# One transfer, two issuers: the row of the maxima leaves from ScalarE instead of SyncE in an attention and feed-forward kernel

## The chip, the cores and the metric

The kernel runs on one core of a Trainium2 chip. The metric is the device time of one execution in microseconds. A program is timed over whole executions; the profile shows one of them, with the span from its first to its last instruction. Five engines work side by side, each with its own order of instructions: TensorE (PE), VectorE (DVE), ScalarE (ACT), GpSimd (POOL) and SyncE (SP), which here only issues transfers. They wait for each other through semaphores.

## The reference, cut to what matters

```python
def layernorm(x): return (x - mean(x)) / sqrt(var(x) + 1e-5)

def attention(x, W_qkv, b_qkv, W_out, b_out):      # x: 32 x 256 x 128 (batch, position, feature)
    q, k, v = split(x @ W_qkv + b_qkv)             # 16 query heads and 4 key/value heads of 8
    scores = einsum('bkgsd,bktd->bkgst', q, k) / sqrt(8)   # 4 query heads share one key head
    scores = where(causal, scores, -inf)
    return (softmax(scores) @ v) @ W_out + b_out

def ffn(x, weight, alpha, bias):                   # weight made ternary: -1, 0, 1
    return x @ (ternary(weight) * alpha).T + bias

x = x + layernorm(attention(layernorm(x)))
x = x + layernorm(ffn(layernorm(x)))
```

## The kernel before

The 32 batch elements ("batches") are taken one after the other, each with 256 positions of 128 features in two halves of 128 rows. The stages of a batch are spread over many steps: each engine has a function `step(t)` that lists, in a fixed order written by hand, the pieces of work that it does in step t, for batches of different age (`exp(t - 3, 0)`, `norm(t - 8, ...)`). Each piece starts with the semaphores that it waits for. Nothing else sets the order: an engine, and the queue of the transfers that it issues, goes through its list from top to bottom.

What a batch b goes through, as far as it matters here:

1. ACT copies the turned input from PSUM (`xn1T`, L488). PE makes queries and keys of it (L916), ACT takes them with their bias (`QK`, L495 and L496).
2. Queries and keys are cut into three bfloat16 parts (`part1` on ACT, L456; `rest` on GpSimd, L400; `part2` on ACT, L463; `part3` on GpSimd, L378), and SP sends these parts into the stacks `QS` and `KS` (L260 and L270), six transfers for QS and three for KS a batch. Four batches have stacks of their own (`RING = 4`).
3. PE multiplies the stacks once for the maxima (`mx`, L846); DVE reduces them (`maxima`, L627) to the largest score of each query within a head. DVE and GpSimd make a high and a low bfloat16 part of it (`Mp`, L690 and L392), PE turns them (`turn`, L886), and ACT copies the result to `MpT` (`take_turned`, L470). MpT is a single buffer of 16 x 512.
4. A transfer, `send_max` (L278), puts MpT, 16 KB, into the last two rows of the stack QS. With those rows the scores product gives scores with the maxima already subtracted.
5. PE makes the scores (`st`, L795); its first piece for a batch waits for `s_mrow`, the semaphore of that transfer. ACT takes the exponentials (`exp`, PT, L427), PE multiplies them by the values (`pv`, L819), ACT copies the sums (`Y`, L449).
6. The divisors: SP sends them out of Y to `den` (L286), DVE inverts them (`rec`, L699), SP stores them to DRAM (`rec_dram`, L294) and loads them back, spread over the rows (`rden`, L301, 256 KB). GpSimd multiplies (`yn`, L386), PE makes the output product (L875), DVE adds the bias and takes the moments.
7. The attention's layer norm is applied by ACT in place of DVE (`norm(b, 1, ...)`, A, L440, two instructions of 128 x 128), with a shift and a scale that GpSimd computes (`shift`, L362). The feed-forward part follows later (x3, ff, `norm(b, 3, ...)`, F, the same line).

SP's order around the maxima is `load_x`, `spread_rec`, `send_max`, then the remaining parts of Q and K. So `send_max` stands behind the load of rden, which waits until rec_dram has landed. ACT's order at the end of a step is the exponentials 3 and 4, `take_turned(t - 2)`, the norm of A, and then, at the head of the next step, `take_xn1`.

`take_turned` waits for `s_mrow` before it overwrites MpT, and signals `s_mt`, for which the transfer waits. A helper `free` (L208) makes the waits that keep a buffer from being overwritten; each is an instruction of its own on the engine's sequencer.

Of the kernel before, what the change touches and what calls it, by code (L numbers as in the profile page):

```python
# [23 lines left out]
MAXROW = BL + PARTS  # L24
# [4 lines left out]
RING = 4  # L29
# [7 lines left out]
def on(b):  # L37

    return 0 <= b < B
# [23 lines left out]
def build(nc, x, wq, wk, wv, wo, bq, bk, bo, wf, alpha, bf, ident, qfix, kfix, vmask, bvw, out):  # L63
    with ExitStack() as ctx:
        def sb(name, shape, dt):
            return ctx.enter_context(nc.sbuf_tensor(name, shape, dt))
# [4 lines left out]
        def sem(name):  # L71
            return ctx.enter_context(nc.semaphore(name))
# [37 lines left out]
        QS = [sb(f"QS{i}", [128, NH, S], BF16) for i in range(RING)]  # L110
# [4 lines left out]
        MpT = sb("MpT", [4 * NKV, 2 * S], BF16)  # L115
# [62 lines left out]
        s_mt = sem("s_mt")  # L178
        s_mrow = sem("s_mrow")
# [43 lines left out]
        def _(sp):  # L223
# [17 lines left out]
            def load_x(t):  # L241
                g = t + 1
                if g < B // GRP:

                    sp.wait_ge(s_x, g * 16)
                    load(g)
# [6 lines left out]
            def q_rows(b, part, c):  # L253
                if on(b):
                    i = b % RING
                    src = (part1, part2, part3)[part][i]

                    sp.wait_ge((s_p1, s_p2, s_p3)[part], b + 1)
                    r = BL + HD * c
                    sp.dma_start(QS[i][r:r + HD, :, :], src[:, 0, :]).then_inc(s_stack[i], 16)  # L260
# [10 lines left out]
                                 src[0:32 * n, 1, :].unsqueeze(1).broadcast_to([32 * n, COPIES, S]))\  # L271
                      .then_inc(s_stack[i], 16)

            def send_max(b):
                if on(b):

                    sp.wait_ge(s_mt, b + 1)
                    sp.dma_start(QS[b % RING][MAXROW:MAXROW + 2, :, :], MpT[:]).then_inc(s_mrow, 16)  # L278

            def send_den(b):  # L280
                if on(b):
                    i = b % 2

                    sp.wait_ge(s_y, b + 1)
                    free(sp, b, s_rec, bufs=2)
                    sp.dma_start(den[i][:], Y[i][HD:128:2 * HD].rearrange("r a s -> r (a s)")).then_inc(s_den[i], 16)  # L286
# [9 lines left out]
            def spread_rec(b):  # L296
                if on(b):
                    i = b % 2

                    second(sp, b, s_recd[i])  # L300
                    sp.dma_start(rden[i][:].rearrange("r a s -> r (a s)"),  # L301
                                 rec_dram[i].unsqueeze(1).broadcast_to([8, 16, NLO * S])).then_inc(s_shift[i], 16)
# [12 lines left out]
            def step(t):  # L315
                load_x(t)
                spread_rec(t - 5)
                send_max(t - 3)
                q_rows(t - 1, 1, 1)
                q_rows(t - 1, 1, 5)  # L320
                k_rows(t - 1, 2)
                q_rows(t - 1, 2, 0)
                store_x(t - 21)
                send_den(t - 4)
                rows_free(t)
                q_rows(t, 0, 2)
                q_rows(t, 0, 3)
                q_rows(t, 0, 4)
                store_rec(t - 4)
                k_rows(t, 0)  # L330
                k_rows(t, 1)

            for t in range(B + 21):
                step(t)
# [82 lines left out]
        @block.scalar  # L417
        def _(act):
            def exp(b, n):
                if not on(b):  # L420
                    return
                banks = ST_CHUNKS[n][2]

                act.wait_ge(s_st_ps, CHUNKS * b + n + 1)
                if b * CHUNKS + n >= TILES:
                    act.wait_ge(s_pv, CHUNKS * b + n - TILES + 1)
                nc.scalar.activation(PT[(b * CHUNKS + n) % TILES][:, 0:512 * banks],  # L427
                                     ps_st[n % 2][:, 0:banks, :].rearrange("p a c -> p (a c)"),
                                     ACT.Exp, scale=SCALE).then_inc(s_exp, 1)

            def norm(b, k, src, dst, done, added):

                if not on(b):
                    return

                i = b % 2
                act.wait_ge(s_rstd[k], 3 * b + 3)
                free(act, b, added, bufs=2)
                for j in range(TT):
                    last = nc.scalar.activation(dst[i][:, j, :], src[i][:, j, :], ACT.Identity, bias=shift[k][i][:, j:j + 1],  # L440
                                                scale=rstd[k][i][:, j:j + 1])
                last.then_inc(done, 1)

            def take_y(b):
                if on(b):

                    act.wait_ge(s_pv, CHUNKS * b + CHUNKS)
                    free(act, b, s_yn, bufs=2)
                    nc.scalar.copy(Y[b % 2][:], ps_y[:]).then_inc(s_y, 1)  # L449

            def first_part(b):
                if on(b):

                    act.wait_ge(s_qk, 2 * b + 2)
                    stack_sent(act, b, RING)
                    nc.scalar.copy(part1[b % RING][:], QK[:]).then_inc(s_p1, 1)  # L456

            def second_part(b):
                if on(b):

                    act.wait_ge(s_r1, b + 1)
                    stack_sent(act, b, RING)
                    nc.scalar.copy(part2[b % RING][:], rest[:]).then_inc(s_p2, 1)  # L463

            def take_turned(b):
                if on(b):

                    act.wait_ge(s_mt_ps, b + 1)
                    free(act, b, s_mrow, 16)
                    nc.scalar.copy(MpT[:].rearrange("r (h i s) -> r i h s", h=2, i=NB),  # L470
                                   ps_w[0:16, :].rearrange("r (i h s) -> r i h s", i=NB, h=2)).then_inc(s_mt, 1)


            def take_v(b):
                if on(b):

                    act.wait_ge(s_v_ps, b + 1)
                    free(act, b, s_pv, CHUNKS, RING)
                    nc.scalar.copy(VB[b % RING][:, :, 0:HD],
                                   ps_w[:, 0:128].rearrange("p (n c) -> p n c", c=HD)).then_inc(s_vb, 1)  # L480

            def take_xn1(b):
                if on(b):

                    act.wait_ge(s_xt_ps, b + 1)
                    free(act, b, s_v_ps)
                    free(act, b, s_qk_ps)
                    nc.scalar.copy(xn1T[:], ps_w[:, 0:S]).then_inc(s_xt, 1)  # L488

            def take_qk(b):  # L490
                if on(b):

                    act.wait_ge(s_qk_ps, b + 1)
                    free(act, b, s_r1)
                    nc.scalar.activation(QK[:, 0, :], ps_w[:, 0:S], ACT.Identity, bias=bq_sb[:, 0:1]).then_inc(s_qk, 1)  # L495
                    nc.scalar.activation(QK[:, 1, :], ps_w[:, S:2 * S], ACT.Identity,  # L496
                                         bias=bk_sb[:, 0:1]).then_inc(s_qk, 1)

            def take_xn3(b):
                if on(b):  # L500

                    act.wait_ge(s_x3_ps, b + 1)
                    free(act, b, s_ff_ps)
                    nc.scalar.copy(xn3T[:], ps_w[:, 0:S]).then_inc(s_x3, 1)

            for dst, src in ((id_sb, ident), (wk_sb, wk), (bq_sb, bq), (bk_sb, bk)):
                act.dma_start(dst[:], src).then_inc(s_early, 16)
            for dst, src in ((wv_sb, wv), (vm_sb, vmask)):
                act.dma_start(dst[:], src).then_inc(s_vconst, 16)
            for dst, src in ((wo_sb, wo), (bv_sb, bvw), (bo_sb, bo)):  # L510
                act.dma_start(dst[:], src).then_inc(s_late, 16)
            act.wait_ge(s_setg, 1)
            for i in range(RING):
                act.dma_start(KS[i][MAXROW:ROWS], neg[:].unsqueeze(1).broadcast_to([2, NKV, KLEN])).then_inc(s_neg, 16)

            act.wait_ge(s_early, EARLY)
            def step(t):
                take_xn1(t)
                exp(t - 4, 5)
                take_qk(t)  # L520
                take_y(t - 4)
                take_xn3(t - 7)
                first_part(t)
                exp(t - 3, 0)
                take_v(t)
                exp(t - 3, 1)
                exp(t - 3, 2)
                norm(t - 8, 3, F1, F2, s_f2, s_fin)
                second_part(t)
                exp(t - 3, 3)  # L530
                exp(t - 3, 4)
                take_turned(t - 2)
                norm(t - 5, 1, A1, A2, s_a2, s_x1)

            for t in range(B + 8):
                step(t)
# [488 lines left out]
```

## Time and profile before

| | us |
|---|---|
| median of 3 runs | 444.55 (444.14 to 447.34) |
| the profiled execution's own time | 445.07 |
| its span | 442.9 |
| PE busy | 374.9 (85%) |
| DVE busy | 359.0 (81%) |
| ACT busy | 329.3 (74%) |
| POOL busy | 300.2 (68%) |

The profiled execution is 0.52 us above the median. Between its span and its own time lie 2.2 us. A batch takes some 11 to 12 us in the middle of the kernel; the first batches and the last ones, where the stages fill and drain, have other limits.

In what follows PEq, ACTq and SPq are the sequencers of the engines: they issue transfers and carry out waits, and their time isn't counted as busy. PEld is the weight load of TensorE, which runs beside its products.

### The profile page before, as it was taken

The page shows a single profiled execution, that of the slowest core. Times are in us where ns is not written, and L with a number is a line of the kernel's source. Part 1 is how long each engine was busy: PE and PEld are TensorE (multiplying, and loading weights), DVE is VectorE, ACT ScalarE, POOL GpSimd, SP SyncE. Part 2 cuts the span into 40 slices and gives each one's busy share as a digit, 9 for nine tenths or more (in the row PEclk, how much of TensorE's full clock was granted, in tenths as well). Part 3 has the DMA queues.
Part 4 walks back from the last instruction along what each step waited for, and adds up shares of the span by engine and source line. Part 5 has one row for each costly group of instructions (what it writes and reads, how often), then busy time and mean ns, then how long its engine had stood idle before and what let it go on. Part 6 is the DMA issues. An engine that isn't in the chain of part 4 may idle for free.

```text
span 442.9 us, 19241 instructions
## 1 busy us (share of the span) xinstructions
PE 374.9 (85%) x7430; PEld 279.5 (63%) x7430; DVE 359.0 (81%) x1148; ACT 329.3 (74%) x609; POOL 300.2 (68%) x584
## 2 busy tenths in 40 slices
PE   0617897999999889999999999999999998798631
PEld 0414676777667667777777767777677776575320
DVE  5378784989989898998999989898899987785542
ACT  0412784888888888898988989898888998668521
POOL 2423332667877777787887878887787777556765
PEclk9967996999999999999999999999999999999865
DMA  5275542454544444433334334443444343311151
GB/s 148 39 89 73 95 88 64 108 107 108 109 106 98 96 104 107 87 80 85 74 83 90 72 88 96 85 105 82 95 87 107 84 108 83 90 30 57 48 170 47
DMA packets 72530, 39.58 MB, mean 89 GB/s; under 512 B 13272, under 2 KB 68280, under 8 KB 72440
## 3 DMA queue, kind: packets, MB, share of 16 engines
q1 hardware_dynamic: 71104, 37.70, 39.9%
q8 instruction: 59, 0.97, 1.0%
q10 hardware_dynamic: 1336, 0.66, 0.6%
q14 instruction: 31, 0.25, 0.2%
HBM read 13.67 MB, written 4.72 MB: 42 GB/s over the span
## 4 chain that ended last, share of the span: by engine, by line
PE 34%; DMA 30%; SPq 11%; DVE 8%; issue 7%; ACT 6%; POOL 3%; POOLq 0%; ACTq 0%; DVEq 0%
DMA QS<-MpT 15%; PE ps_st L795 8%; PE ps_mx L846 7%; DMA den<-Y 7%; PE ps_y L819 7%; DMA rec_dram<-rec 5%; SPq L270 4%; PE ps_w L875 3%; PE ps_w L916 3%; SPq L260 3%; DVE M L627 3%; ACT PT L427 2%; PE ps_w L905 2%; SPq L301 2%; DMA QS<-part 1%
## 5 line engine op out<-in xcount | busy, mean ns | idle before, releaser
L627 DVE TENSOR_REDUCE M<-ps_mx 128x2 f32<-128x512 f32 (+3 forms) x352 | 212.0, 633 | 26.0 <-PE ps_mx L846 25.5
L427 ACT ACTIVATE PT<-ps_st 128x1024 f32<-128x1024 f32 (+1 forms) x192 | 162.6, 884 | 27.3 <-PE ps_st L795 21.6
L846 PE MATMUL ps_mx<-KS,QS 112*64 112x128 bf16 (+2 forms) x2560 | 137.0, 225 | 12.8 <-DMA QS<-part 6.7
L846 PEld LDWEIGHTS ps_mx<-KS,QS 112*64 112x64 bf16 x2560 | 94.0, 112 | 46.7 <-DVE M L627 16.8
L795 PE MATMUL ps_st<-QS,KS 114*64 114x256 bf16 (+1 forms) x1024 | 103.6, 304 | 17.4 <-DMA QS<-MpT 16.8
L358 POOL TENSOR_TENSOR rstd<-vareps,mhalf 128x2 f32<-128x2 f32 x128 | 91.8, 717 | 10.0
L819 PE MATMUL ps_y<-PT,VB 128*32 128x256 f32 (+3 forms) x2048 | 90.5, 303 | 0.4 <-ACT PT L427 0.3
L795 PEld LDWEIGHTS ps_st<-QS,KS 114*64 114x64 bf16 x1024 | 48.5, 111 | 24.5 <-DMA QS<-MpT 22.0
L819 PEld LDWEIGHTS ps_y<-PT,VB 128*32 128x32 f32 x2048 | 49.7, 109 | 12.8 <-issue 6.1
L386 POOL TENSOR_TENSOR yn<-Y,rden 128x512 f32<-128x512 f32 x32 | 40.7, 1270 | 15.8 <-DMA rden<-rec_dram 15.6
L592 DVE BATCH_NORM_STATS2 stats<-X 128x6 f32<-128x128 f32 x128 | 30.7, 281 | 23.8 <-POOL X L370 12.0
L400 POOL TENSOR_TENSOR rest<-QK,part 128x512 f32<-128x512 f32 x32 | 37.1, 1159 | 13.8 <-ACT part L456 13.7
L610 DVE TENSOR_SCALAR xn<-X,mv,rstd 128x128 f32<-128x128 f32 x128 | 40.8, 359 | 3.1 <-PE ps_w L896 2.8
L356 POOL TENSOR_TENSOR vareps<-mv,eps 128x2 f32<-128x2 f32 x128 | 25.4, 198 | 24.2 <-DVE mv L602 23.9
L875 PE MATMUL ps_w<-wo_sb,yn 128*64 128x128 f32 x512 | 36.1, 287 | 4.3 <-POOL yn L386 4.1
L392 POOL TENSOR_TENSOR Mp<-M,Mp 128x32 bf16<-128x32 f32 x32 | 7.8, 245 | 45.1 <-DVE Mp L690 45.0
L378 POOL TENSOR_TENSOR part<-rest,part 128x512 bf16<-128x512 f32 x32 | 37.1, 1159 | 1.5 <-ACT part L463 1.5
L440 ACT ACTIVATE A<-A,shift,rstd 128x128 f32<-128x128 f32 x64 | 28.1, 485 | 11.6 <-POOL shift L362 10.8
L495 ACT ACTIVATE QK<-ps_w,bq_sb 128x256 f32<-128x256 f32 x32 | 15.2, 475 | 26.8 <-PE ps_w L916 26.8
L875 PEld LDWEIGHTS ps_w<-wo_sb,yn 128*64 128x64 f32 x512 | 29.6, 145 | 5.2 <-POOL yn L386 5.1
L602 DVE BATCH_NORM_AGGREGATE mv<-stats 128x2 f32<-128x6 f32 x256 | 30.8, 162 | 0.7
L440 ACT ACTIVATE F<-F,shift,rstd 128x128 f32<-128x128 f32 x64 | 28.0, 491 | 3.5 <-POOL shift L362 3.5
(63 smaller groups left out, 489.7 us busy)
## 6 DMA issues: line engine op xcount, KB each, us to landing
QS<-part SPq DMA_DIRECT2D x192, 64.0 KB
rden<-rec_dram SPq DMA_DIRECT2D x32, 256.0 KB
X<-in_x SPq DMA_DIRECT2D x15, 256.0 KB, 4.4
out<-X SPq DMA_DIRECT2D x15, 256.0 KB, 3.8
KS<-part SPq DMA_DIRECT2D x32, 96.0 KB
KS<-part SPq DMA_DIRECT2D x32, 64.0 KB
KS<-part SPq DMA_DIRECT2D x32, 32.0 KB
QS<-MpT SPq DMA_DIRECT2D x32, 16.0 KB
```

Of the source, the lines that this page charges most:

```text
L358: gp.tensor_tensor(rstd[k][i][:], vareps[k][i][:], mhalf[:], ALU.pow).then_inc(s_rstd[k], 1)
L378: gp.tensor_tensor(part3[i][:], rest[:], part2[i][:], ALU.subtract).then_inc(s_p3, 1)
L386: gp.tensor_tensor(yn[i][:], Y[i][:], rden[i][:], ALU.mult).then_inc(s_yn, 1)
L400: gp.tensor_tensor(rest[:], QK[:], part1[b % RING][:], ALU.subtract).then_inc(s_r1, 1)
L427: nc.scalar.activation(PT[(b * CHUNKS + n) % TILES][:, 0:512 * banks], ps_st[n % 2][:, 0:banks, :].rearrange("p a c -> p (a c)"), ACT.Exp, ...
L440: last = nc.scalar.activation(dst[i][:, j, :], src[i][:, j, :], ACT.Identity, bias=shift[k][i][:, j:j + 1], scale=rstd[k][i][:, j:j + 1])
L610: last = nc.vector.tensor_scalar(dst[i][:, j, :], src(j), mv[k][i][:, j, 0:1], rstd[k][i][:, j:j + 1], ALU.subtract, ALU.mult)
L627: nc.vector.tensor_reduce(M[b % 2][:].rearrange("p k g i -> p (k g) i")[:, 2 * kv:2 * kv + pairs, i], ps_mx[(b * BANKS + n) % 2][:, 0:pair ...
L795: last = pe.matmul(dst[64 * hi:64 * hi + 64, SLOT * slot:SLOT * (slot + nj)], k[:, 2 * hi + lo, key_block(i, diag), :], q[:, j:j + nj, h:h ...
L819: last = pe.matmul(ps_y[32 * g:32 * g + 32, lo, BL * i:S], v[:, at:at + 2, :].rearrange("p a c -> p (a c)"), p[:, g, slot:slot + NB - i, : ...
L846: last = pe.matmul(ps_mx[(b * BANKS + n) % 2][64 * one:64 * one + 64, at:at + w], q[:, h, BL * i:BL * i + BL], k[:, kv, blocks, :], start= ...
L875: last = pe.matmul(ps_w[h:h + 64, D * j:D * j + D], y[:, lo, 128 * j + h:128 * j + h + 64], wo_sb[:, lo, :], start=(lo == 0), stop=(lo == ...
```

## The change

`send_max` goes from SP's program to ACT's. In SP's step it is taken out between `spread_rec(t - 5)` and `q_rows(t - 1, 1, 1)`. In ACT's step it is added as the last piece, behind the norm of A: in the same step in which ACT copies MpT, with the two instructions of the norm between the copy and the transfer. Its wait (`s_mt`), its bytes, its destination and its semaphore stay as they are. No other piece moves.

```diff
@@ SP
-            def send_max(b):
-                if on(b):
-
-                    sp.wait_ge(s_mt, b + 1)
-                    sp.dma_start(QS[b % RING][MAXROW:MAXROW + 2, :, :], MpT[:]).then_inc(s_mrow, 16)
-
@@ SP, step
                 load_x(t)
                 spread_rec(t - 5)
-                send_max(t - 3)
                 q_rows(t - 1, 1, 1)
                 q_rows(t - 1, 1, 5)
                 k_rows(t - 1, 2)
@@ ACT
+            def send_max(b):
+                if on(b):
+
+                    act.wait_ge(s_mt, b + 1)
+                    act.dma_start(QS[b % RING][MAXROW:MAXROW + 2, :, :], MpT[:]).then_inc(s_mrow, 16)
@@ ACT, step
                 take_turned(t - 2)
                 norm(t - 5, 1, A1, A2, s_a2, s_x1)
+                send_max(t - 2)
```

ACT's order after the change, from the copy of one batch's MpT to the copy of the next Y (names as above, the engine's waits in brackets, the numbers at the end are shapes):

```order
L463 CAST MpT<-ps_w 16x4x2x64 [waits s_mrow,s_mt_ps]
L433 ACTIVATE A_0<-A_0,shift_0,rstd_0 128x128 [waits s_x1,s_rstd1]
L433 ACTIVATE A_0<-A_0,shift_0,rstd_0 128x128
L471 DMA QS<-MpT 2x8x512 [waits s_mt]
L487 COPY xn1T<-ps_w 128x256 [waits s_qk_ps,s_v_ps,s_xt_ps]
L420 ACTIVATE PT<-ps_st 128x512 [waits s_pv,s_st_ps]
L494 ACTIVATE QK<-ps_w,bq_sb 128x256 [waits s_r1,s_qk_ps]
L495 ACTIVATE QK<-ps_w,bk_sb 128x256
L442 COPY Y<-ps_y 128x512 [waits s_yn,s_pv]
```

The same piece before the change:

```order
L470 CAST MpT<-ps_w 16x4x2x64 [waits s_mrow,s_mt_ps]
L440 ACTIVATE A_0<-A_0,shift_0,rstd_0 128x128 [waits s_x1,s_rstd1]
L440 ACTIVATE A_0<-A_0,shift_0,rstd_0 128x128
L488 COPY xn1T<-ps_w 128x256 [waits s_qk_ps,s_v_ps,s_xt_ps]
L427 ACTIVATE PT<-ps_st 128x512 [waits s_pv,s_st_ps]
```

Only the row of the transfer is new; the line numbers differ for the same work because a function moved in the file.

SP's order before the change, from the store of one batch's inverted divisors to the sending of the next den:

```order
L294 DMA rec_dram<-rec 128x32 [waits s_yn,s_rec]
L270 DMA KS<-part_3 24x8x256 [waits s_p1]
L270 DMA KS<-part_3 16x8x256 [waits s_p2]
L231 DMA X<-in_x 128x4x128 [waits s_x]
L301 DMA rden<-rec_dram 128x1x512 [waits s_recd1]
L278 DMA QS<-MpT 2x8x512 [waits s_mt]
L260 DMA QS<-part_3 8x16x256 [waits s_p2] x2
L270 DMA KS<-part_3 8x8x256 [waits s_p3]
L260 DMA QS<-part_3 8x16x256 [waits s_p3]
L286 DMA den<-Y 128x1x32 [waits s_rec,s_y]
```

After it:

```order
L288 DMA rec_dram<-rec 128x32 [waits s_yn,s_rec]
L270 DMA KS<-part_3 24x8x256 [waits s_p1]
L270 DMA KS<-part_3 16x8x256 [waits s_p2]
L231 DMA X<-in_x 128x4x128 [waits s_x]
L295 DMA rden<-rec_dram 128x1x512 [waits s_recd1]
L260 DMA QS<-part_3 8x16x256 [waits s_p2] x2
L270 DMA KS<-part_3 8x8x256 [waits s_p3]
L260 DMA QS<-part_3 8x16x256 [waits s_p3]
L280 DMA den<-Y 128x1x32 [waits s_rec,s_y]
```

The maxima no longer stand between the load of rden and the second parts of Q; the rest keeps its order.

## Rows read from the trace of the kernel before

**Rows 1.** Waits of the whole span: engine, line, releaser, us in total, times, longest
```profile
PE ps_st L795 <- DMA QS<-MpT: 16.8, 19, 2.7
```

**Rows 2.** The page, part 4: the chain that ended last, by line, share of the span
```profile
DMA QS<-MpT 15%; PE ps_st L795 8%; PE ps_mx L846 7%; DMA den<-Y 7%; PE ps_y L819 7%; DMA rec_dram<-rec 5%; SPq L270 4%; PE ps_w L875 3%; PE ps_w L916 3%; SPq L260 3%; DVE M L627 3%; ACT PT L427 2%; PE ps_w L905 2%; SPq L301 2%; DMA QS<-part 1%
```

**Rows 3.** Waits of the stretch 89.91 to 367.20 us, columns as in the first group
```profile
ACT QK L495 <- PE ps_w L916: 12.7, 24, 0.7
...
PE ps_st L795 <- DMA QS<-MpT: 8.8, 14, 1.4
...
DVE rec L699 <- DMA den<-Y: 5.9, 10, 1.4
...
ACT A L440 <- POOL shift L362: 0.3, 1, 0.3
```

**Rows 4.** Busy time by stretch (from the end of one copy of MpT to another)
```profile
core 0: us, PE busy (x) PEld busy (x) DVE busy (x) ACT busy (x) POOL busy (x), PEclk, DMA share, GB/s
241.66:252.53 10.87, 10.86 (x238) 8.52 (x232) 10.57 (x36) 9.99 (x20) 9.25 (x19) 1.00 0.38 84
252.53:264.49 11.96, 11.07 (x236) 8.51 (x232) 10.53 (x36) 10.13 (x21) 9.12 (x19) 1.00 0.32 79
...
89.91:367.20 277.29, 266.91 (x5576) 202.79 (x5568) 252.60 (x826) 243.16 (x455) 218.68 (x424) 1.00 0.43 94
```

**Rows 5.** Timeline of ACT, 241 to 244 us: start, duration, line, output<-input, idle before
```profile
241.10 0.56 ACT L470 CAST MpT<-ps_w 16x512 bf16<-16x512 f32 x1
241.56 0.88 ACT L440 ACTIVATE A<-A,shift,rstd 128x128 f32<-128x128 f32 x2
242.35 0.37 ACT L488 COPY xn1T<-ps_w 128x256 f32<-128x256 f32 x1
...
243.99 0.47 ACT L495 ACTIVATE QK<-ps_w,bq_sb 128x256 f32<-128x256 f32 x1 [0.52 <-PE ps_w L916]
```

**Rows 6.** Timeline of PE in the same batch: its first scores product
```profile
245.56 0.60 PE L795 MATMUL ps_st<-QS,KS 114*64 114x256 bf16 x6
```

**Rows 7.** The chain, 184 to 208 us; the last row is ACT's timeline
```profile
188.94 3.28 DMA den<-Y
...
192.63 2.96 DMA rec_dram<-rec
...
195.60 0.62 SPq L301
...
196.26 4.33 DMA QS<-MpT
...
195.26 0.56 ACT L470 CAST MpT<-ps_w 16x512 bf16<-16x512 f32 x1
```

**Rows 8.** The page, part 6: transfers of 16 KB, median us to landing at the end
```profile
rec_dram<-rec SPq DMA_DIRECT2D x32, 16.0 KB, 2.0
```

**Rows 9.** Timeline of SP in the batch of the fifth group
```profile
241.68 0.67 SPq L278 DMA_DIRECT2D QS<-MpT  x1
```

**Rows 10.** The wait of L208 in 264.30 to 264.38 us; timeline of ACT there
```profile
L208 ACTq EVENT_SEMAPHORE  x1: 38/38/38, 264.3 to 264.3; - x1
...
263.93 0.56 ACT L470 CAST MpT<-ps_w 16x512 bf16<-16x512 f32 x1
264.39 0.87 ACT L440 ACTIVATE A<-A,shift,rstd 128x128 f32<-128x128 f32 x2
265.35 0.37 ACT L488 COPY xn1T<-ps_w 128x256 f32<-128x256 f32 x1
```

**Rows 11.** Timeline of ACT and SP at the kernel's start: issues only
```profile
0.74 0.45 ACTq L507 DMA_DIRECT2D id_sb<-in_ident  x1
...
5.18 3.27 ACTq L514 DMA_DIRECT2D KS<-neg  x4
...
0.74 0.45 SPq L233 DMA_DIRECT2D X<-in_x  x1
```

**Rows 12.** Timeline of POOL and PE, 258 to 261 us
```profile
258.65 1.27 POOL L386 TENSOR_TENSOR yn<-Y,rden 128x512 f32<-128x512 f32 x1 [1.54 <-DMA rden<-rec_dram]
...
259.98 1.09 PE L875 MATMUL ps_w<-wo_sb,yn 128*64 128x128 f32 x16
```

## The prediction

> **What bounds the kernel now.** I read the waits, the chain, the busy times of two neighbouring batches, and then one batch in the timeline. Shares of the span say little where four engines hand the same batch to each other, so the first look is at who ends the idle time. TensorE stood still for 16.8 us in 19 places at L795, the scores product, for one transfer: QS<-MpT, the row of the maxima [rows 1]. That transfer is also 15% of the chain [rows 2]. This is the object of the change, and it is a real wait.
>
> How much of it is steady state? In the stretch 89.91 to 367.20 us there are 24 batches (ACT waits once in each for the query product, 24 times), and 8.8 of the 16.8 us lie there, in 14 waits [rows 3]. The windows give the price of one: a batch without it lasted 10.87 us, the next one, with it, 11.96 us; the mean of the 24 is 277.29 / 24 = 11.55 us [rows 4]. In the short batch PE is busy 10.86, DVE 10.57 and ACT 9.99 us of 10.87 [rows 4], so about 10.9 us is a floor that a cheaper transfer can't break.
>
> The reader should then see a batch at close range. ACT ends the copy of MpT at 241.10 + 0.56 = 241.66 us, the norm of A runs behind it until 242.44, and xn1T begins at 242.35, without a gap [rows 5]. TensorE comes to the first scores product at 245.56, which is 3.90 us after the copy's end [rows 6]. That is the due time of the transfer: whatever lands later than copy + 3.9 stops TensorE, and behind it ACT's first exponential.
>
> The transfer misses it for two reasons, both to be seen in one piece of the chain [rows 7]. First the issue: den<-Y, the reciprocal, rec_dram<-rec and then the SP issue of L301 (rden) run until 196.22, and only then does SP issue the maxima, at 196.26, though their copy ended at 195.82. The maxima stand in SP's order behind a load that waits for another chain. The same difference, taken from the two rows of each of the 32 batches, adds up to about 10 us; in half of them it is under 0.05. Second the landing: 4.33 us for 16 KB, when the same number of bytes of rec_dram<-rec has a median of 2.0 us [rows 8]. Ahead of the maxima on SP's queue lie the 256 KB of rden, issued 0.66 us before.
>
> **The change part by part.**
> Removed from SP: 32 issues of 0.67 us [rows 9], of a batch of 11.5 us. SP isn't waited for in most of that time, so I cost the relief at nothing by itself; what it moves (the parts of Q and K, then den<-Y, all up to 0.7 us earlier) can only help the den chain.
>
> Issue time. ACT's transfer waits for ACT's own copy, and for SP's neighbour no more. It stands behind both instructions of the norm. Does the sequencer reach it only when they have ended, 0.8 us after the copy, or before? The trace shows it for another instruction in the same place: the wait of L208 that stands behind both norm instructions and ahead of xn1T ran at 264.3 us [rows 10], while the copy of that batch ran to 264.49 and the norm began at 264.39. So ACT's sequencer is ahead of its engine by the norm, and I take the issue at copy + 0.05, as early as SP's best (241.66 to 241.68 [rows 5, 9]). If the norm's shift from GpSimd is late, the transfer is late with it; a wait of the norm for the shift was large enough to be listed once in 24 batches, with 0.3 us [rows 3].
>
> Landing time. No trace of this kernel shows this transfer on ACT's queue with rden on the other. The bounds are 2.0 us (rec_dram<-rec, [rows 8]) and 4.33 (the same transfer now, [rows 7]). I take 3.2, in the middle: the 256 KB no longer stand in front, but the same engines move them. Landing is then at copy + 0.05 + 3.2 = copy + 3.25, ahead of the 3.90 of TensorE. At 4.33 it would be copy + 4.4, half a microsecond late in every batch.
> The Trainium skill, DMA: Bandwidth & Descriptors, section Issuing engines are not separate DMA queues, speaks against the gain in landing: transfers of all issuers interleave on the same engines, and another issuer saves only issue time. By that alone the landing stays near 4.3, and the result is the third case below; the lower row of 2.0 us doesn't decide it, since nothing large was ahead of that transfer.
>
> Gain: all 8.8 us of the steady waits, which leaves 11.55 - 8.8 / 24 = 11.2 us a batch, above the floor; and of the 16.8 - 8.8 = 8.0 us in the ramps half, 4.0, since other waits stand beside them there. Together 12.8 us.
>
> Cost on ACT. An issue of this kind takes about 0.65 us of the sequencer: 0.67 on SP [rows 9], and on ACT the four small KS<-neg took 3.27 us, waits included, so at most 0.82 each [rows 11]. It hides under the norm, 0.88 us in the engine [rows 5]: from copy + 0.05 to copy + 0.73, then the waits of xn1T. xn1T now begins 0.69 us after the copy in the short batch (242.35 - 241.66), so it slips by some 0.1 to 0.15 in these, and not at all where it begins at copy + 0.86 (265.35 - 264.49 [rows 10]), as it does in about half of the batches. 30 batches x 0.07 = 2 us, all on the path: qk follows xn1T, and ACT is nearly dense from there on. If the cover were gone the price would be 0.67 + 0.04 = 0.71 us a batch.
> At the kernel's start ACT and SP issue side by side, 0.45 us each from 0.74 on [rows 11], so I add nothing for a collision of the two issuers. The Trainium skill, Perfetto Trace Analysis, section DMA Instruction - HWDGE, says that the block that makes descriptors is locked for one sequencer at a time; if ACT had to wait out an issue of SP, about 0.6 us more would stand on ACT, which is near the price without cover.
>
> What is late next: rden itself. In one slow batch GpSimd waited 1.54 us for it and began yn at 258.65; TensorE's L875 followed at 259.98, straight behind its 1.27 us [rows 12]. With the batch shortened by 0.9 us that chain would stop TensorE instead. Four of the 24 batches look like this, some also wait for den (5.9 us of DVE in all [rows 3]). I give back 2 us.
>
> Sum: - 12.8 + 2.0 + 2.0 = - 8.8 us. The profiled execution took 445.07 us, so 436.3; it lies 0.5 above the median of 444.55, which gives 435.8, say 436.
>
> **The rivals.**
> *The den chain takes over.* SP no longer gates the maxima, but den, rec, rec_dram and rden still run one after the other: 3.28 + 2.96 us in transfers alone [rows 7]. If each shortened batch meets it, only a third of the 12.8 is left: - 4 us, 440.5. For it: DVE waited for den in 10 of the 24 batches [rows 3]. Against: in the short batches this chain was in time, and its transfers now leave earlier.
> *The landing stays.* With 4.33 us the transfer wins only the delay of its issue. Batch by batch that is worth the smaller of the delay and of TensorE's wait; I took both from the timeline for the batches with a wait and got 7.5 us; less 2 on ACT is - 5.5: 439.
> *More than forecast.* The den chain gets faster too and the batches come to 11.0: 24 x 0.55 + 4 + some = - 15: 430. All ramps gone as well gives 424 at the very least; I stop at 429.
> *Slower: ACT stands still for its issue.* If ACT's engine gets nothing while its sequencer issues, or the issue comes only after the norm, 0.71 us lie between norm and xn1T in every batch. ACT has no slack there: it is busy without a gap from the copy to xn1T, and its idle time before QK, 0.52 us [rows 5], waits for a product of xn1T and moves with it. 29 x 0.71 = 20.6 against 12.8 is + 8; by the floor, 11.0 + 0.71 against 11.55, it is + 4 in the steady part. Between them + 6: 450.5. It decides from about 0.36 us a batch on, where 30 of them eat the net 10.8. For it: no ACT row shows an issue between two activations. Against: the wait that ran ahead of the norm [rows 10].
>
> **How the numbers follow.** Forecast as summed 50%, more 8%, landing stays 15%, den chain 12%, slower 15%. The likeliest gives 436. The range 429 to 444 leaves out the slower case and a little beneath. One per cent, about what a measurement of this kernel can tell from no change, is 440.1 and 449.0. Faster by more: 50 + 8 + most of the third case + a third of the den case = 0.71; slower by more: most of the last, 0.12; the rest, 0.17, within.
>
> **What the profile after would show.** Right: QS<-MpT issued by ACTq within 0.1 us of the copy's end, while the norm runs; the wait of L795 for it nearly gone from 16.8 us; xn1T at copy + 0.8 to 0.9 everywhere; steady batches of about 11.2 us; and DVE's wait for den or GpSimd's for rden as the largest of the transfers. Wrong: an issue after the norm's end, or xn1T at copy + 1.4, is the slower case; a wait at L795 that stays at 0.5 us in each batch means the queue was not what delayed the landing; batches of 11.4 with more than 15 us of waits for den and rden mean that the bound only moved.

## The result: slower, and the profile after

The changed kernel takes 461.31 us (459.69 to 465.63, 4 runs) against 445.94 us before (444.14 to 447.48): the ratio is 1.044, with an interval of 1.037 to 1.051. The prediction was 436 us, range 429 to 444. The profiled execution took 465.63 us, with a span of 463.5 us. It is the slowest of the four, 4.3 us above their median, so its span grew by 20.6 us where the medians differ by 15.4.

First the wait that was to vanish. The waits of the changed kernel, whole span (engine, line, releaser, us in total, times, longest):

```profile
DVE M L627 <- PE ps_mx L846: 44.7, 50, 2.2
...
ACT PT L420 <- PE ps_st L795: 37.0, 37, 2.5
PE ps_st L795 <- DMA QS<-MpT: 30.4, 28, 2.1
...
POOL yn L379 <- DMA rden<-rec_dram: 14.2, 8, 4.3
```

TensorE now waits 30.4 us for the maxima, not 16.8 [rows 1]. DVE and ACT wait behind it, and the waits for rden haven't grown. In part 4 of the profile's page, the same transfer is a quarter of the chain, instead of 15% [rows 2]:

```profile
DMA QS<-MpT 25%; PE ps_st L795 8%; ACT PT L420 7%; PE ps_mx L846 6%; PE ps_y L819 4%; PE ps_w L875 3%; ACT F L433 3%; DMA QS<-part 2%; ACT MpT L463 2%; PE ps_w L916 2%; SPq L260 2%; PE ps_w L861 2%; POOL rstd L351 2%; PE ps_w L905 1%; DVE M L627 1%
```

The same 24 batches as in [rows 4], again from copy to copy (stretch, us, busy times):

```profile
core 0: us, PE busy (x) PEld busy (x) DVE busy (x) ACT busy (x) POOL busy (x), PEclk, DMA share, GB/s
241.06:252.87 11.81, 11.13 (x238) 8.51 (x232) 10.67 (x36) 10.19 (x20) 9.33 (x19) 1.00 0.39 79
...
93.40:386.75 293.35, 269.62 (x5576) 205.40 (x5568) 255.14 (x825) 244.29 (x455) 219.71 (x424) 0.99 0.44 88
```

293.35 against 277.29 us is 16.1 of the 20.6 us by which the span grew: 12.22 us a batch instead of 11.55. Of the rest, 2.8 us lie between the first copy of MpT and the fifth, and about 2 us behind the last one.

Then one batch at close range, which answers to [rows 5, 9]. ACT's timeline, with its transfer, and SP's of the same time:

```profile
240.50 0.56 ACT L463 CAST MpT<-ps_w 16x512 bf16<-16x512 f32 x1
240.97 0.49 ACT L433 ACTIVATE A<-A,shift,rstd 128x128 f32<-128x128 f32 x1
241.09 0.62 ACTq L471 DMA_DIRECT2D QS<-MpT  x1
241.36 0.48 ACT L433 ACTIVATE A<-A,shift,rstd 128x128 f32<-128x128 f32 x1
241.83 0.37 ACT L487 COPY xn1T<-ps_w 128x256 f32<-128x256 f32 x1
...
239.52 0.62 SPq L295 DMA_DIRECT2D rden<-rec_dram  x1
240.18 1.27 SPq L260 DMA_DIRECT2D QS<-part  x2
241.85 0.72 SPq L270 DMA_DIRECT2D KS<-part  x1
...
245.12 0.63 SPq L280 DMA_DIRECT2D den<-Y  x1
```

The issue on ACT is all that was hoped for: 0.03 us after the copy's end (241.06), between the two instructions of the norm, with xn1T at copy + 0.77. But SP has sent two copies of Q's second part, 128 KB, at 240.18: 0.9 us *ahead* of the maxima. Before, SP waited for the maxima's copy, because it had to send them, and these parts left only behind that. The chain and TensorE's timeline show the end of that transfer:

```profile
241.09 4.75 DMA QS<-MpT
...
245.88 0.62 PE L795 MATMUL ps_st<-QS,KS 114*64 114x256 bf16 x6 [0.68 <-DMA QS<-MpT]
```

Means over the 24 batches, from the records of the issues, of the packets and of the semaphore in the trace: the first copy of Q's second part left 1.00 us after the maxima's copy before, and in none of the 24 ahead of it; now 0.41 us ahead of the copy's end, and in 19 of 24 ahead of or with the maxima. The last packet of the maxima ran 2.72 us after their issue before, 3.78 now. They landed 3.83 us after the issue before, 4.97 now; from the copy, 4.12 before and 5.01 now. The growth lies in the packets: the first one begins 2.57 us after the issue instead of 2.14, and the 16 of them then take 1.21 us from the first start to the last instead of 0.57, with packets of the parts between them; the tail behind the last start hardly changed (1.11 and 1.19). TensorE comes to its first scores product 4.1 us after the copy in the mean of both kernels (3.90 was the batch of [rows 6]); that product began 4.47 us after the copy before and begins 5.11 after it now. These 0.64 us are nearly all of the 0.67 us by which a batch grew.

### The profile page after: what moved, and what is told of

It reads as the page before. It is cut to its first block, busy times and chain, and to the rows that moved or that the text cites. A ratio compares the mean times of both kernels' runs of the same rounds, so it can differ in the third digit from the quotient of the medians.

```text
span 463.5 us, 19241 instructions
## 1 busy us (share of the span) xinstructions
PE 384.8 (83%) x7430; PEld 286.9 (62%) x7430; DVE 361.8 (78%) x1148; ACT 330.6 (71%) x609; POOL 299.5 (65%) x584
## 3 DMA queue, kind: packets, MB, share of 16 engines
HBM read 13.67 MB, written 4.72 MB: 40 GB/s over the span
## 4 chain that ended last, share of the span: by engine, by line
DMA 30%; PE 29%; ACT 14%; issue 12%; DVE 5%; POOL 5%; SPq 3%; POOLq 0%; ACTq 0%; DVEq 0%
DMA QS<-MpT 25%; PE ps_st L795 8%; ACT PT L420 7%; PE ps_mx L846 6%; PE ps_y L819 4%; PE ps_w L875 3%; ACT F L433 3%; DMA QS<-part 2%; ACT MpT L463 2%; PE ps_w L916 2%; SPq L260 2%; PE ps_w L861 2%; POOL rstd L351 2%; PE ps_w L905 1%; DVE M L627 1%
## 5 line engine op out<-in xcount | busy, mean ns | idle before, releaser
L846 PE MATMUL ps_mx<-KS,QS 112*64 112x128 bf16 (+2 forms) x2560 | 139.6, 229 | 11.6 <-DMA QS<-part 6.0
L795 PE MATMUL ps_st<-QS,KS 114*64 114x256 bf16 (+1 forms) x1024 | 106.0, 309 | 30.7 <-DMA QS<-MpT 30.4
L846 PEld LDWEIGHTS ps_mx<-KS,QS 112*64 112x64 bf16 x2560 | 97.7, 115 | 44.8 <-DVE M L627 11.8
L351 POOL TENSOR_TENSOR rstd<-vareps,mhalf 128x2 f32<-128x2 f32 x128 | 90.2, 705 | 10.0
L795 PEld LDWEIGHTS ps_st<-QS,KS 114*64 114x64 bf16 x1024 | 48.6, 113 | 40.9 <-DMA QS<-MpT 38.6
L875 PE MATMUL ps_w<-wo_sb,yn 128*64 128x128 f32 x512 | 37.2, 293 | 5.0 <-POOL yn L379 5.0
L875 PEld LDWEIGHTS ps_w<-wo_sb,yn 128*64 128x64 f32 x512 | 30.8, 149 | 6.0 <-POOL yn L379 5.9
L348 POOL TENSOR_TENSOR nmean<-mv,minus 128x2 f32<-128x2 f32 x64 | 12.7, 199 | 27.6 <-DVE mv L602 27.6
```

The costliest lines, as they stand in the source:

```text
L351: gp.tensor_tensor(rstd[k][i][:], vareps[k][i][:], mhalf[:], ALU.pow).then_inc(s_rstd[k], 1)
L795: last = pe.matmul(dst[64 * hi:64 * hi + 64, SLOT * slot:SLOT * (slot + nj)], k[:, 2 * hi + lo, key_block(i, diag), :], q[:, j:j + nj, h:h ...
L846: last = pe.matmul(ps_mx[(b * BANKS + n) % 2][64 * one:64 * one + 64, at:at + w], q[:, h, BL * i:BL * i + BL], k[:, kv, blocks, :], start= ...
L875: last = pe.matmul(ps_w[h:h + 64, D * j:D * j + D], y[:, lo, 128 * j + h:128 * j + h + 64], wo_sb[:, lo, :], start=(lo == 0), stop=(lo == ...
```

## The experiments

Two theories could explain the late landing. A: the transfers that SP now sends ahead of the maxima, or with them, delay them. B: a transfer on ACT's queue is slower beside bulk on SP's, whatever the order. C, ACT's time for the issue, was the slower rival of the prediction. "Landing" below is the mean over the same 24 batches from issue to the last increment of the semaphore. Times are compared with the kernel before on the same chip, which gave 447.26, 443.34 and 444.73 us in the three groups of runs.

**Only the issuer changed.** SP gets its wait back, but sends nothing there.

```diff
+            def hold(b):
+                if on(b):
+                    sp.wait_ge(s_mt, b + 1)
                 spread_rec(t - 5)
+                hold(t - 3)
```

> The changed kernel, but SP waits for s_mt where send_max stood, and sends nothing there. So the parts of Q and K again leave behind the copy of the maxima, and only the issuer differs from the kernel before. Theory A (lost order: in the changed kernel SP no longer waits for the copy, its part copies leave up to 0.9 us ahead of the maxima and share the engines with them): landing back to at most 3.9 us from the issue (4.9 in the changed kernel), TensorE's wait at L795 under 17 us, time 446 or less. Rival B (other queue: beside a queue that carries rden, the ACT queue gives the maxima only a share, whatever the parts do): landing stays at 4.7 to 5 us, time 455 to 462. Rival C (ACT's issue costs ACT time): landing falls but the time stays above 455, with xn1T as in the changed kernel.

Measured: 454.67 us, ratio 1.019 (1.008 to 1.030); landing 4.72 us, TensorE's wait 21.6 us. Neither theory's numbers: a wait alone gives back about half of the loss, while the landing falls by only 0.25 us. ACT and SP in one batch show why it isn't the old order:

```profile
187.43 0.62 ACTq L476 DMA_DIRECT2D QS<-MpT  x1
...
187.43 1.27 SPq L260 DMA_DIRECT2D QS<-part  x2
```

Both are released by the same copy and go at the same instant. Before, SP's own issue of the maxima, 0.67 us long [rows 9], stood between, so the maxima had a lead of 0.72 us.

**The maxima first, from SP and from ACT.** In the first kernel SP's order of before is turned round; in the second the changed kernel's SP waits for s_mt ahead of rden.

```diff
-                spread_rec(t - 5)
                 send_max(t - 3)
+                spread_rec(t - 5)
```

> The kernel before, with send_max ahead of spread_rec on SP: the maxima no longer stand behind the 256 KB of rden, but rden waits for the copy of the maxima. Theory A: with nothing issued ahead of it the transfer lands 2.2 to 2.5 us after its issue, the wait at L795 is nearly gone, and the time falls to 430 to 440 unless rden, up to 1.5 us later, stops GpSimd and the output product. If the waits for rden take over: 442 to 448.

```diff
+                hold(t - 3)
                 spread_rec(t - 5)
```

> The changed kernel, but SP waits for s_mt ahead of spread_rec, so that neither rden nor the parts are ahead of the maxima, which leave from ACT. Theory A: landing 2.3 to 3.0 us from the issue, time as in the kernel with send_max first on SP, plus up to 2 us for ACT's issue: 432 to 445. Rival B: landing above 3.5 us although it was issued first, since the bulk on the other queue overtakes it; time over 445.

Measured: 470.14 us, 1.053 (1.043 to 1.064), landing 2.43 us; and 476.81 us, 1.068 (1.058 to 1.079), landing 5.05 us. The first landed as expected, and the weight loads of L795 wait 1.0 us in all for it, its products 0.2. But the time lies far above both of its ranges: rden and what follows leave late, and the waits move there.

```profile
DVE rec L699 <- DMA den<-Y: 59.6, 31, 3.1
...
POOL yn L386 <- DMA rden<-rec_dram: 43.8, 31, 4.8
```

They were 10.1 and 15.6 us in the kernel before. The second result looks like support for B. Its rows say something else:

```profile
211.03 0.62 SPq L299 DMA_DIRECT2D rden<-rec_dram  x1
...
211.04 0.62 ACTq L476 DMA_DIRECT2D QS<-MpT  x1
...
211.04 5.33 DMA QS<-MpT
```

Rden is released by the same copy and isn't behind but level. By the packets' records the maxima of this batch began 3.31 us after their issue, when the last of rden's 128 packets had just begun (3.30). The place in the order isn't all, though: by then 76 packets of the parts had begun too, which SP had issued 0.66 us and more *behind* the maxima. In the batch at 175.55, equally level, the maxima's packets went first and they landed after 2.3 us. 3 of 24 batches landed in under 3 us. So at a tie one of the two goes first, nearly whole, and it is mostly the large one.

**The parts ahead of the maxima, on one queue.** This is the kernel before with SP's order changed:

```diff
-                send_max(t - 3)
                 q_rows(t - 1, 1, 1)
                 q_rows(t - 1, 1, 5)
+                send_max(t - 3)
```

> The kernel before, with the two copies of the second part of Q ahead of send_max on SP: the order that the changed kernel often has, but on one queue. Theory A: the landing of the maxima grows, through the two copies in front and the later issue (0.67 us each), to at least 1 us more after the copy than before; the wait at L795 is 30 us or more, time 458 to 470. Rival B: the one queue keeps the landing itself at about 3.9 us from its issue; only a late issue costs, and where SP reaches the parts before the copy of the maxima is done it costs nothing: 444 to 452.

Measured: 492.4 us, 1.105 (1.095 to 1.116); landing 4.69 us from an issue that itself came 0.88 us after the copy; TensorE waits 47.2 us. The time is above what A allowed, but the landing is A's and not B's 3.9: one queue doesn't protect the maxima from what stands in front.

**ACT's transfer with nothing in front.** The changed kernel and the kernel before, each with the two copies of Q's second part behind send_den.

```diff
-                q_rows(t - 1, 1, 1)
-                q_rows(t - 1, 1, 5)
                 k_rows(t - 1, 2)
                 q_rows(t - 1, 2, 0)
                 store_x(t - 21)
                 send_den(t - 4)
+                q_rows(t - 1, 1, 1)
+                q_rows(t - 1, 1, 5)
```

> The changed kernel with the two copies of the second part of Q moved behind send_den on SP, so that 128 KB less are in flight beside the maxima; rden still is. Theory A (the transfers that SP issues around the maxima delay them): landing from 4.97 to about 3.8 us from the issue, the wait at L795 under 12 us, time 440 to 450. Rival B (the other queue alone): landing over 4.5 us, time over 455.

> The kernel before with the same two copies moved behind send_den. On one queue they stood behind the maxima anyway. Theory A: the landing itself falls a little (3.83 to about 3.5 us from the issue) and den, with less in front of it, lands earlier: 436 to 446. If the late copies stop the next batch's maxima (TensorE at L846 waiting for QS<-part): above 450.

Measured: 480.56 us both, 1.086 (1.077 to 1.096) and 1.084 (1.070 to 1.097). Both are slow for the reason that the second expectation names: TensorE's maxima product waits for the late parts, 49.3 us in the first (waits of that kernel) and 26.0 in the second:

```profile
PE ps_mx L846 <- DMA QS<-part: 49.3, 30, 6.3
```

For the question the first of them is the clearest run. SP falls behind, so that rden leaves 0.64 us *after* the copy in the mean, and in 22 of 24 batches the maxima go ahead of it:

```profile
222.32 0.62 ACTq L471 DMA_DIRECT2D QS<-MpT  x1
...
222.99 0.62 SPq L295 DMA_DIRECT2D rden<-rec_dram  x1
```

They landed after 2.57 us on average, and 2.23 us in this batch, from ACT's queue, with 256 KB starting on SP's 0.67 us later. From SP's queue with nothing in front it was 2.43 (the kernel with send_max first). B is wrong: ACT's queue is as fast, if its transfer is issued first. In the second kernel, where rden stays ahead on SP's queue, the landing was 3.51 us, as expected, but from an issue 1.25 us after the copy.

**SP waits for the landing.** As the first experiment, with this wait instead:

```diff
+                    sp.wait_ge(s_mrow, 16 * b + 16)
```

> The changed kernel, but SP waits where send_max stood until the maxima have landed. Then rden alone is beside them. Theory A: landing about 3.0 to 3.6 us from the issue, no wait at L795 beyond the first and last batches; the parts and den leave up to 2 us later, so the time is set by those: 445 to 460. Rival B: landing stays at 4.5 us or more, time 465 or more.

Measured: 509.33 us, 1.150 (1.140 to 1.161), far above what A allowed, but the landing is 3.06 us with rden alone around it: 0.73 us ahead of the copy on average, nearly as before (0.65). What was 3.83 us is 3.06 without the parts behind, and 0.5 of these 0.77 us lie between the start of the last packet and the semaphore (1.1 us before, 0.6 here). So what is issued 0.7 us behind the maxima costs them something too. The time goes to SP, which waits 99.4 us for the landings; den leaves 6.1 us after the copy instead of 4.3.

**ACT's issue without cover.** The changed kernel with send_max ahead of the norm.

```diff
                 take_turned(t - 2)
+                send_max(t - 2)
                 norm(t - 5, 1, A1, A2, s_a2, s_x1)
-                send_max(t - 2)
```

> The changed kernel with send_max directly behind the copy on ACT, ahead of the norm. The issue can't come earlier than in the changed kernel (0.03 us after the copy), but the norm, pushed behind it, loses its cover: it begins 0.7 us after the copy instead of 0.1 before it, and xn1T 1.4 to 1.6 us after the copy instead of 0.79. If ACT's order is on the path, the period of the steady batches grows by up to the 0.7 us where the landing isn't the later of the two (xn1T leads to TensorE's first scores product 3.2 us later), so by less than 0.3 us here: 461 to 470. If the sequencer's time were what made the changed kernel slow, this one would be at 480.

Measured: 463.43 us, 1.049 (1.041 to 1.057), within the expected range. ACT's timeline:

```profile
237.68 0.56 ACT L463 CAST MpT<-ps_w 16x512 bf16<-16x512 f32 x1
238.27 0.62 ACTq L471 DMA_DIRECT2D QS<-MpT  x1
238.99 0.88 ACT L433 ACTIVATE A<-A,shift,rstd 128x128 f32<-128x128 f32 x2 [0.75 <-ACT MpT L463]
239.78 0.35 ACT L487 COPY xn1T<-ps_w 128x256 f32<-128x256 f32 x1
```

The norm is held up by 0.75 us, and xn1T begins at copy + 1.55 instead of 0.79 (means). That is the price without cover, and it is real. The time hardly moves because the delay hides behind the late landing: in the 14 batches without a wait TensorE now comes to its first scores product at copy + 4.80, by when the maxima, at copy + 4.66 in the mean, have landed, and its waits at L795 fall from 30.4 to 9.4 us; that product begins at copy + 5.03, against 5.11 in the changed kernel. C is not what made the changed kernel slow, since there xn1T begins as early as in the kernel before (0.79). With an earlier landing the uncovered issue would be on the path; that was not tried.

**A lead for the maxima again.** SP keeps the wait of the first experiment and sends the third parts, which are ready some 0.8 us after the copy, ahead of the second. The same order with SP as the issuer is the control.

```diff
-                q_rows(t - 1, 1, 1)
-                q_rows(t - 1, 1, 5)
                 k_rows(t - 1, 2)
                 q_rows(t - 1, 2, 0)
+                q_rows(t - 1, 1, 1)
+                q_rows(t - 1, 1, 5)
```

> The changed kernel with SP's wait for s_mt put back and SP's four part copies in another order: the third parts of K and Q (ready some 0.8 us after the copy of the maxima) ahead of the second parts of Q. So the maxima, sent by ACT, have 0.7 us of lead over everything but rden, as they had before, where their own issue on SP gave it. If the missing lead is what kept the kernel with the wait alone at 4.72 us of landing: landing 3.9 or less, landing from the copy 3.9 or less (4.12 before), steady batches 11.5 or less, time 438 to 447. If the lead doesn't matter: landing 4.5 to 4.8, time 450 to 456.

> The kernel before with the same new order of the four part copies, as the control for the kernel that sends from ACT with that order. The maxima have a lead of 0.7 us with either order here, so the landing stays at 3.6 to 3.9 us and the time within 1% of before: 440 to 449. What the ACT version gains over this one is the issue alone (0.04 against 0.28 us after the copy).

Measured: 450.02 us, 1.013 (1.000 to 1.026), landing 3.44; the control 448.17 us, 1.011 (0.999 to 1.023), landing 3.57. The lead came out larger than the 0.7 us of the expectation: in the ACT version the next copy, the 32 KB of K, leaves 1.14 us behind the maxima in most batches, and the second parts of Q 2.6 us behind them. With such a lead ACT's transfer lands as early as SP's, and 3.52 us after the copy, earlier than in the kernel before (4.12). TensorE waits for it 4.4 us in the whole span. The time doesn't fall below the kernel before all the same. The waits of the ACT version in its 24 batches:

```profile
DVE rec L704 <- DMA den<-Y: 26.0, 23, 2.3
...
PE ps_w L910 <- DVE A L679: 7.8, 17, 1.2
```

DVE's wait for den was 5.9 us in 10 waits before [rows 3], and it is 22.1 us in 23 waits in the control, so it comes with the order of the parts, which now stand closer in front of den, and not with the issuer. The gain at the maxima is given back there: the steady batches take 11.92 us, where 11.5 or less was expected, and no less than with SP's wait alone. ACT's version and the control don't differ beyond their intervals.

**The second parts a step earlier**, at the end of SP's step and ahead of rden, with no wait for the maxima.

```diff
-                q_rows(t - 1, 1, 1)
-                q_rows(t - 1, 1, 5)
...
                 k_rows(t, 1)
+                q_rows(t, 1, 1)
+                q_rows(t, 1, 5)
```

> The changed kernel with the two second parts of Q sent a step earlier, at the end of SP's step, ahead of rden, without any wait of SP for the maxima. These copies and rden are then in front of the maxima and nothing but the third parts, 0.8 us later, behind. If the order of issue over both queues sets the landing, the transfer still waits out what is in front: landing 4.0 to 4.8 us, time 445 to 460, slower than with the parts behind. If only what is issued at the same instant or after hurts: landing under 3.9, time 436 to 446.

Measured: 480.06 us, 1.081 (1.066 to 1.095), landing 4.77. The landing is what A said, though rden was ahead of the maxima in only 10 of the 24 batches: in these they landed after 5.30 us in the mean, in the other 14, with the parts in front and rden level or behind, after 4.39. The time is beyond the range, because rden now leaves 0.19 us after the copy instead of 0.65 before it, and GpSimd waits 52.5 us for it.

## Why the prediction was wrong, step by step

**The step that failed is the landing time**, "Landing is then at copy + 0.05 + 3.2 = copy + 3.25". It measured 4.97 from the issue and 5.01 from the copy. The bounds, 2.0 and 4.33 us, were taken from transfers in the old order of issue, and the upper one was treated as a ceiling. The 4.33 had 256 KB in front and the parts behind; in the new order the parts are in front too. The premise of the 3.2, "the 256 KB no longer stand in front", failed as well: rden left 1.11 us ahead of the copy in the mean (0.65 before), and when the first packet of the maxima began, 119 or more of rden's 128 packets had begun in 23 of the 24 batches. The error behind it is in the sentence on SP: what it moves, "all up to 0.7 us earlier", "can only help the den chain". The wait that was removed from SP wasn't only idle time for SP. It kept 128 KB from leaving ahead of 16 KB that TensorE needs sooner. Two experiments price it: with SP's wait back the steady batches take 11.90 us (285.69 us for 24) instead of 12.22, and with a lead over all the parts as well the landing is 3.44 us.

**The gain** of 12.8 us at L795 was a loss of 13.6 (16.8 to 30.4). In the 24 steady batches 8.8 us of waits were to go to nothing and became 22.7.

**The issue time was right**: 0.04 us after the copy in the mean of the 24 batches, 0.05 forecast, 0.28 before. ACT's sequencer does run ahead of its engine, as [rows 10] said.

**ACT's cost** was forecast at 2 us; the mean start of xn1T is 0.79 us after the copy in both kernels, so it was about nothing. The price without cover, 0.71 forecast, is 0.75 us a batch. A collision of the two issuers, which the prediction left out of its sum, didn't show either: ACT's issue took 0.65 us at most in the 24 batches, also where SP issued at the same instant.

**The rivals.** "The landing stays" had the landing nearest to what was measured, and the Trainium skill's sentence ahead of it pointed the same way; I gave it 15% and held the landing at 4.33 us, so it too came out faster than before (439). By the Trainium skill, DMA: Bandwidth & Descriptors, section Issuing engines are not separate DMA queues, the transfers of all issuers interleave on the same engines. The runs agree that a second issuer buys no priority: 5.05 us level with rden, 2.57 ahead of it. The slower case, with 15%, came out on the right side and for the wrong reason, so that was luck. The den chain as the next bound was right in kind: it is what holds the ACT version with a lead at 450 us, and the version with the maxima first at 470.

**What stays open** is how the engines share packets in detail. In most batches the maxima's packets begin only when rden's have nearly all begun, on either queue (3.31 us against 3.30 in the batch shown); with the parts they mix. Why transfers issued shortly behind the maxima lengthen the tail from the last packet to the semaphore (1.1 us, against 0.6 without them) is not shown.

One thing I overlooked, and no run varies it: these transfers don't seem to use all 16 DMA engines. The semaphore of the maxima takes 3 updates a transfer, that of rden 9, and that of rec_dram<-rec, from which the 2.0 us came, 16; and in the middle of the kernel, before and after the change, there are never more than 4 packets of the maxima or 12 of rden in flight, but up to 24 of all transfers together. As an estimate from these counts, the maxima run on about 2 engines and rden on about 8, which would make the place behind rden costlier than its bytes suggest. Whether rden spread over more engines would let the maxima land earlier is open.

## What to carry to other kernels

A wait in a queue of transfers also orders traffic: before moving a transfer off a queue, list what its wait was holding back, and expect all of that to leave ahead of it. What counts for a small transfer that an engine is waiting for is what is issued ahead of it and shortly behind it, over all queues, and not its own queue: here it lands after 2.2 to 2.6 us with nothing in front, 3.1 behind 256 KB alone, 3.8 with the parts 0.7 us behind it as well, and 5.0 with the parts in front too. A lead of 1.1 us over the next copy, and of 2.6 us over the 128 KB, brought the landing from 4.72 to 3.44 us; an issuer of its own brought nothing that could be measured.

## What the hardware showed that I had not expected

Two transfers on two queues, issued at the same instant (within 0.05 us in 23 of 24 batches), don't share evenly: in the batch shown, the packets of the 16 KB came after all of the 256 KB had begun, and in most batches they landed as late (5.05 us on average); in 3 of 24 they landed in under 3 us. And an issue of 0.63 us on ACT costs its engine nothing if it comes while two instructions of 0.88 us together run, as in the changed kernel, while the same issue directly behind a copy, with the norm behind it in the order, keeps the engine idle for 0.75 us.
